# Graph attention and product-key attention on one core: a second set of gathered rows moves from GpSimd to ScalarE's queue

## The reference

```python
x = x + _L0_gnn_ref(_layernorm(x), adj, W, a)
x = x + _L0_ffn_ref(_layernorm(x), Wq_pk, pk_keys, Wq, keys_table, values_table, Wo)

def _L0_ffn_ref(x, ...):
    q = (x @ Wq).reshape(b, n, HEADS, DIM) * DIM ** (-0.5)
    kv_scores, indices = _pk(x, Wq_pk, pk_keys)      # 16 rows of 16384 for each token and head
    ind = indices + offsets[None, None, :, None]
    k = jnp.einsum('bnhk,bnhkd->bnhd', kv_scores, keys_table[ind])
    v = jnp.einsum('bnhk,bnhkd->bnhd', kv_scores, values_table[ind])
    sim = jnp.where(causal, jnp.einsum('bihd,bjhd->bhij', q, k), neg)
    attn = jax.nn.softmax(sim, axis=-1)
    out = jnp.einsum('bhij,bjhd->bhid', attn, v)
    return out.transpose(0, 2, 1, 3).reshape(b, n, HEADS * DIM) @ Wo
```

## Time and profile before

| | |
|---|---|
| median of three runs | 10136.64 us (10135.63 to 10138.01) |
| span of the profiled execution | 10159.7 us; the page gives no time for that execution besides |
| GpSimd busy | 7625.7 us, 75% |
| VectorE busy | 6962.0 us, 69% |
| TensorE busy (matmuls) | 5615.2 us, 55% |
| ScalarE busy | 3117.0 us, 31% |
| gathers | 8003, of 953 ns |
| granted TensorE clock, mean | 0.728 |

### The profile page before, as it was taken

One profiled execution on the slowest core, in us unless ns is written; L12 is line 12 of the kernel. 1 busy time (PEld: TensorE's weight loads), 2 busy tenths in 40 slices (PEclk: granted clock), 3 DMA queues, 4 the chain that ended last, 5 costly groups with the idle time before them and its releaser, 6 DMA issues.

```text
span 10159.7 us, 173542 instructions
## 1 busy us (share of the span) xinstructions
PE 5615.2 (55%) x23108; PEld 4511.4 (44%) x23108; DVE 6962.0 (69%) x42780; ACT 3117.0 (31%) x9770; POOL 7625.7 (75%) x8020
## 2 busy tenths in 40 slices
PE   5655555555555555555555555555555555555555
PEld 4544444444444444444444444444444444444444
DVE  8866667666666667666776666766667676666663
ACT  4333233332333333333333233333333333322222
POOL 5777777777777777777777777777777777777776
PEclk7777777777777777777777777777777777777777
DMA  3333333333333333333333333333333333333333
GB/s 109 104 108 108 108 112 108 108 108 108 112 108 107 108 108 112 108 108 108 108 112 108 108 108 108 112 108 108 107 110 110 108 108 108 108 110 108 108 108 99
DMA packets 481297, 1099.25 MB, mean 108 GB/s; under 512 B 180864, under 2 KB 222720, under 8 KB 479968
## 3 DMA queue, kind: packets, MB, share of 16 engines
q0 software_dynamic: 384144, 1049.48, 36.1%
q1 hardware_dynamic: 71152, 31.60, 1.2%
q10 hardware_dynamic: 24800, 8.19, 0.4%
HBM read 1084.36 MB, written 4.19 MB: 107 GB/s over the span
## 4 chain that ended last, share of the span: by engine, by line
POOL 73%; issue 24%; DVE 2%; PE 1%; POOLq 0%; DMA 0%; ACT 0%; ACTq 0%; SPq 0%; DVEq 0%
POOL ring L346 73%; DVE hot L998 0%; PE ps_o L709 0%; DMA wo<-in_Wo 0%; DVE ps_v L920 0%; POOLq L362 0%; PE ps_p L595 0%; POOLq L360 0%; DMA ring<-in_table,idx 0%; PE ps_p L599 0%; ACTq L483 0%; PE ps_s L681 0%; DVE nmax L1049 0%; PE ps_w L656 0%; DVE edge L849 0%
## 5 line engine op out<-in xcount | busy, mean ns | idle before, releaser
L346 POOL DMA_INDIRECT ring<-in_table,idx x8003 | 7624.1, 953 | 2507.7 <-issue 2440.8
L656 PE MATMUL ps_w<-ring,diag 128*128 128x256 f32 x8192 | 1996.2, 400 | 9.7 <-DMA ring<-in_table,idx 9.6
L700 PE MATMUL ps_p<-ident,prob 128*128 128x128 f32 x2304 | 548.8, 390 | 2576.1 <-ACT prob L446 2568.1
L656 PEld LDWEIGHTS ps_w<-ring,diag 128*128 128x128 f32 x8192 | 1630.3, 205 | 244.8 <-issue 12.7
L917 DVE TENSOR_SCALAR ps_v<-ring,wgt 128x256 f32<-128x256 f32 x512 | 248.7, 486 | 2147.8 <-DMA ring<-in_table,idx 2147.8
L998 DVE SCALAR_TENSOR_TENSOR hot<-rank,posf,cand 128x54 f32<-128x54 f32 x8192 | 1655.4, 270 | 0.3
L700 PEld LDWEIGHTS ps_p<-ident,prob 128*128 128x128 f32 x2304 | 371.4, 194 | 2769.7 <-ACT prob L446 1734.0
L920 DVE SCALAR_TENSOR_TENSOR ps_v<-ring,wgt,ps_v 128x256 f32<-128x256 f32 x3072 | 1478.1, 481 | 19.6
L437 ACT ACTIVATE diag<-ident,wgt 128x128 f32<-128x128 f32 x4096 | 1251.9, 391 | 0.0
L668 PE MATMUL ps_t<-ident,kv 128*128 128x128 f32 x512 | 234.4, 458 | 1642.4 <-DVE kv L931 1642.4
L709 PEld LDWEIGHTS ps_o<-probT,kv 128*128 128x128 f32 x4608 | 1040.8, 318 | 145.9 <-ACT probT L454 69.9
(11 more groups left out here) (119 smaller groups left out, 8053.9 us busy)
## 6 DMA issues: line engine op xcount, KB each, us to landing
far<-in_table SPq DMA_DIRECT2D x16256, 1.0 KB
ring<-in_table,idx POOLq DMA_INDIRECT x8003
far<-in_table ACTq DMA_DIRECT2D x7936, 1.0 KB
xin<-in_x SPq DMA_DIRECT2D x8, 512.0 KB, 4.6
mask<-in_adj SPq DMA_DIRECT2D x1, 4096.0 KB, 14.6
out_x<-acc SPq DMA_DIRECT2D x64, 64.0 KB
far_row<-far_at SPq DMA_DIRECT2D x127, 0.5 KB
far_row<-far_at ACTq DMA_DIRECT2D x62, 0.5 KB
```

What stands on the lines that cost most here:

```text
L346: pool.indirect_dma_start(out=ring[:, t % RING, k, :], out_offset=None, in_=table, in_offset=bass.IndirectOffsetOnAxis(ap=idx[:, t, k:k + ...
L656: ins = nc.tensor.matmul(pw_ps, diag[:, k, :], ring[:, t % RING, k, :], start=(k == 0), stop=(k == PE_ROWS - 1))
L700: ins = nc.tensor.transpose(ps_p[:, c, (j % 4) * P:(j % 4 + 1) * P], prob[:, j * P:(j + 1) * P], ident[:])
```

## The change

Unit 4's last row becomes a set too. `NEAR` becomes (0, 4), and ScalarE fetches both: set 0 of head n + 1 in units 1 to 4 of head n, set 4 in units 5, 6, 7 and in unit 0 of the next head, 32 transfers in each unit. In each unit the load of 32 addresses and the first 8 transfers (`HIDDEN`) now stand right behind the diagonals, ahead of oT and qT; the other 24 stand where the transfers stood before. GpSimd's looped head has 124 gathers. For head 1, SyncE fetches set 0, set 3, three quarters of set 4 and set 7 in this order; before, it fetched set 0, then 3 and 7.

```diff
-NEAR = 0
-NEAR_ROWS = (0, 20, 20, 20, 20, 16, 16, 16)
-SETS = FAR + (NEAR,)
+NEAR = (0, 4)
+SETS = FAR + NEAR
+NEAR_UNITS = 4
 FAR_ROW = TOPK - 1
 LOADED = 32
+HIDDEN = 8
...
             load(1)
             far_begin(1, last_set + 1)
+            far_fetch(1, last_set + 1)
             far_begin(1, 0)
-            far_fetch(1, last_set + 1)
-            with sp.Fori(1, HEADS) as h:
+            far_begin(1, last_set + 2)
+            far_fetch(1, 0)
+            far_begin(1, 1)
+            far_fetch(1, last_set + 2, P - LOADED)
+            far_begin(2, 0)
+            far_fetch(1, 1)
+            with sp.Fori(2, HEADS) as h:
                 far_sets(h, range(len(FAR)))
...
-            def near_fetch(n, part):
-
-                if NEAR_ROWS[part - 1] == 0:
-                    act.wait_ge(far_row_dma[near], n * 16)
+            def near_load(n, i, part):
+
+                if part in (0, NEAR_UNITS - 1):
+                    act.wait_ge(far_row_dma[i], n * 16)
                     act.sem_inc(act_mark, 1)
-                    act.wait_ge(rows_summed, (n - 1) * UNITS + NEAR + 1)
+                    act.wait_ge(rows_summed, (n - 1) * UNITS + SETS[i] + 1)
                     act.sem_inc(act_mark, 1)
...
+            def near_rows(i, part, at, rows):
+                for j in rows:
+                    q = part * LOADED + j
+                    act.dma_start(far[q:q + 1, i, :].bitcast(U8), table_bytes[bass.ds(at[j], KV_BYTES)]) \
+                        .then_inc(far_dma[i], 16)
...
-                    if ahead and t == 1 and not first:
-                        near_begin(n + 1)
+                    if ahead and t in (1, 1 + NEAR_UNITS) and not first:
+                        near_begin(n + 1, len(FAR) + t // NEAR_UNITS)
...
                     elif ahead:
                         diagonals(n + 1, 0)
+                    fetch = not first and (ahead or t == 0)
+                    if fetch:
+                        near = len(FAR) + (t - 1) % UNITS // NEAR_UNITS
+                        part = (t - 1) % NEAR_UNITS
+                        at = near_load(n + 1 if t else n, near, part)
+                        near_rows(near, part, at, range(0, HIDDEN))
                     if t or not first:
                         attend_out(*behind)
...
-                    if ahead and t >= 1 and not first:
-                        near_fetch(n + 1, t)
+                    if fetch:
+                        near_rows(near, part, at, range(HIDDEN, LOADED))
```

More of the change, by code:

```diff
@@ L278, in far_begin, with far_fetch @@
                     sp.dma_start(far_row[0:1, i, :], far_at[:, i:i + 1]).then_inc(far_row_dma[i], 16)
-            def far_fetch(n, i):
+            def far_fetch(n, i, stop=P):
                 sp.wait_ge(far_row_dma[i], n * 16)
@@ L286, in far_fetch @@
                     sp.sem_inc(sp_mark, 1)
-                for q in range(0, P, LOADED):
+                for q in range(0, stop, LOADED):
                     _, at = nc.values_load_multi_w_load_instructions(
@@ L458, in attend_out, with near_begin @@
                 nc.scalar.copy(oT[:], oT_ps).then_inc(o_copied, 1)
-            near = len(FAR)
-            def near_begin(n):
-                act.wait_ge(idx_ready, n * UNITS + NEAR + 1)
+            def near_begin(n, i):
+                act.wait_ge(idx_ready, n * UNITS + SETS[i] + 1)
                 act.sem_inc(act_mark, 1)
                 with nc.allow_non_contiguous_dma(reason="one table address of each token"):
-                    act.dma_start(far_row[0:1, near, :], far_at[:, near:near + 1]).then_inc(far_row_dma[near], 16)
-            def near_fetch(n, part):
-                if NEAR_ROWS[part - 1] == 0:
-                    act.wait_ge(far_row_dma[near], n * 16)
+                    act.dma_start(far_row[0:1, i, :], far_at[:, i:i + 1]).then_inc(far_row_dma[i], 16)
+            def near_load(n, i, part):
+                if part in (0, NEAR_UNITS - 1):
+                    act.wait_ge(far_row_dma[i], n * 16)
                     act.sem_inc(act_mark, 1)
-                    act.wait_ge(rows_summed, (n - 1) * UNITS + NEAR + 1)
+                    act.wait_ge(rows_summed, (n - 1) * UNITS + SETS[i] + 1)
                     act.sem_inc(act_mark, 1)
-                q = sum(NEAR_ROWS[:part])
+                q = part * LOADED
                 _, at = nc.values_load_multi_w_load_instructions(
-                    far_row[0:1, near, q:q + NEAR_ROWS[part]], engines=[mybir.EngineType.Activation],
+                    far_row[0:1, i, q:q + LOADED], engines=[mybir.EngineType.Activation],
                     min_val=0, max_val=(HEADS * NUM_KV - 1) * KV_BYTES,
                     skip_runtime_bounds_check_because="made of two positions below 128 and a head below 8")
-                for j in range(NEAR_ROWS[part]):
-                    act.dma_start(far[q + j:q + j + 1, near, :].bitcast(U8), table_bytes[bass.ds(at[j], KV_BYTES)]) \
-                        .then_inc(far_dma[near], 16)
+                return at
+            def near_rows(i, part, at, rows):
[3 more added lines that the diff above has]
+                        .then_inc(far_dma[i], 16)
             act.wait_ge(aux_mm, 1)
```

## The result

The changed kernel takes 10061.15 us (median of four runs, 10058.81 to 10064.14) where before takes 10137.33 in the same comparison: 76.2 us less, a ratio of 0.9924 (95% interval 0.9912 to 0.9936). The forecast was 10057.6 us, 79.0 us less than the median it started from.

A forecast was written before the change was run, and what follows sets the result against it. GpSimd's gathers were taken to bound the kernel: 63 gathers go, 79.2 us, and ScalarE's transfers, VectorE's lag and the start cost nothing; 10080.5 us of span, scaled to the runs' median, gives 10057.6 us, range 10045 to 10078.

The forecast's parts named there:

- What bounds, and what goes: GpSimd's stream of gathers bounds; one gather of 1.2576 us goes in each of 63 later heads, 79.2 us.
- The cost of the queue: ScalarE's queue: 128 more transfers a head at 0.31 us and longer address loads, 46.7 us a head if nothing covers it.
- The cover: Load and first 8 transfers run beside the eight diagonals: bounds 0 to 19.6 us a head, some 16 us taken.
- the sum of 135.2 us: ScalarE's looped head from busy time, transfers, loads, probT and loop turn, with all 19.6 us beside the diagonals taken off.
- ScalarE's head: ScalarE's time for a looped head, never waiting for data: 154.8 us uncovered, 135.2 us covered, against GpSimd's 155.9 us.
- So ScalarE stays below it in either case: ScalarE's looped head stays under GpSimd's 155.9 us, by 1 us uncovered or by 21 us covered.
- The two ways of counting agree: Added queue work set against ScalarE's free waits, and its never waiting head summed directly, both leave ScalarE under GpSimd.
- Rival 1: Looped head: ScalarE becomes the bound, uncovered with oT and qT waits kept, 169.5 us a head, 10911 us; chance 0.07.
- VectorE's lag and the ring: VectorE lags 1 to 5 us more in places; ring places free 31 us early at batch turns absorb it, costing nothing.
- Rival 2: Batch turns: VectorE catches up too slowly, GpSimd waits 5 to 10 us at each of 7 turns, 10093 to 10128 us; chance 0.05.
- The start: Head 1: SyncE's reordered fetches land in time, GpSimd's 10.15 us wait before unit 2 stays as it is; cost nothing.
- The smallest slack of all: Head 1: 12 us between the end of unit 0's kv and the gather that needs its ring place.

The follow-up runs named there:

- runs three and nine: Changed kernel with load and all 32 transfers behind qT, nothing behind the diagonals: 10921.2 us; changed kernel with only the load behind the diagonals: 10061.1 us.

## Why the prediction was right, and where not

- **What bounds, and what goes.** Right, and shown: without the fetch 10057, with both gathers and fetch 10138. The term of 79.2 us measured 79.9 in the first of these and 76.2 in the changed kernel. In the profiles the gather shown above at 273.24 us starts at 270.30 in the run without the fetch, which is most of the difference; why stays open.
- **The cost of the queue.** 0.31 us a transfer was right (0.306 when the queue bounds). SyncE's load of 32 numbers was the right row for ScalarE's: median 2144 ns over 497 of them.
- **The cover.** I took most of it, some 16 us a head, and it measured 16.0. But the sum of 135.2 us has 19.6 taken off, not 16; with 16 it would have been 138.8. The Trainium skill (Advanced Engine Details and Errata, Engine Queue Depths) gives the queue a depth of 8. The eight diagonals agree with it; the nine instructions that 74 loads ran ahead of are one more, and the measurement decides.
- **ScalarE's head.** Here the working failed, though the forecast held. "So ScalarE stays below it in either case" was wrong: uncovered it is 169.5 us, not 154.8. The sum had the trip for probT and left out the waits for oT and qT and the one for unit 0's kT. "The two ways of counting agree" proved nothing, since both took these waits for filled. Covered it is 142.0, not 135.2: 14 us of margin, not 21. Rival 1 had the uncovered case right, with 169.5 us a head and 10911 us (measured 10921), because it kept waits beside the transfers. That it hit so closely is luck: it put all 14.7 us on oT and qT, which kept 10.4 in that run (655.4 / 63), and unit 0's kT, which it didn't name, another 4.3. The forecast hung on the load's cover alone (runs three and nine), while I had said that it holds without any.
- **VectorE's lag and the ring.** Right: GpSimd's waits for kv are 12.6 us, all told, its longest issue is 0.3 us, and the slack at the turns is 30.5 us. Rival 2, losses at the turns, is out by the same numbers.
- **The start.** "Stay as they are" was not quite so: the wait of 10.15 us became 12.27. "The smallest slack of all", 12 us at unit 4 of head 1, was misread; unit 3's was 7.2 us in the trace of before, and 7.8 in the changed kernel. With five sets the start cost 13 us.
- **The trace expected after.** 7940 gathers, 15904 transfers, waits of 1777.5 us between 700 and 1900: as said. The eight transfers start less than 3 us after the first diagonal in 462 of 497 cases (median 2.3); the other 35 are all in unit 1, up to 5.75 us. A gather takes 1.2548 us, not 1.257.

## What to carry to other kernels

An engine that is 31% busy can be 9% from being the bound (142.0 us of 155.8, by estimate), when its queue issues transfers: sum its never idle head from issues, loads and the waits that no order fills, and check that sum by loading the queue until it bounds. Issues and loads that stand right behind compute, or ahead of a wait that is there anyway, were nearly free in this kernel; 28 transfers moved were worth 366 us, and the placement decided whether a fifth set gained 65 us or lost 60. A wait can hide under issue, so look at the longest single issue beside its total.

## What the runs showed of the hardware

A load of 32 addresses into registers takes 2.14 us of ScalarE's queue, as much as 7 transfers, and one of 8 takes 0.82 us. It starts while up to nine instructions that stand ahead of it are still to begin (74 of 497 loads of the changed kernel). ScalarE's single transfers did not slow the gathers: a gather cost 1.2548 us with 15904 of them beside it and 1.2546 with 7936 in the run without the fetch. The 1.2576 in the profile of before is that one execution's pace.
